# Self-attention scores as two 64-row tiles in two PSUM banks, with one bank for the output tiles

## The reference

```python
q = (x @ wq).reshape(b, s, 32, 16)      # 32 query heads of width 16
k = (x @ wk).reshape(b, s, 8, 16)       # 8 key groups
v = (x @ wv).reshape(b, s, 8, 16)
k = repeat(k, 4); v = repeat(v, 4)
scores = einsum('bihd,bjhd->bhij', q, k) * 16 ** -0.5
scores = where(causal, scores, min)
out = einsum('bhij,bjhd->bihd', softmax(scores), v).reshape(b, s, 512)
x = x + out @ wo
```

## Time and profile before

| | us |
|---|---|
| median of three runs | 1805.7 (1804.93 to 1806.73) |
| the profiled execution | 1809.07 |
| its span in the profile | 1807.3 |

### The profile page before, as it was taken

How to read it: one execution, slowest core, us unless ns; L and a number is a source line. 1 busy time by engine, 2 the same in 40 slices (tenths; PEclk the granted TensorE clock), 3 DMA queues, 4 the chain that set the end, 5 groups by cost and what they waited for, 6 DMA issues and landing times.

```text
span 1807.3 us, 29658 instructions
## 1 busy us (share of the span) xinstructions
PE 1719.4 (95%) x11352; PEld 1386.4 (77%) x11352; DVE 944.6 (52%) x1657; ACT 749.7 (41%) x1332; POOL 656.1 (36%) x511
## 2 busy tenths in 40 slices
PE   6899899999999999989988998999999999999998
PEld 5556688888888888778974567888888888887797
DVE  4388354544444545574544873544545444446643
ACT  2485344343444444431225753443443434444221
POOL 3396223233242332460115942233232332425500
PEclk9899899999999999999998998999999999999999
DMA  4110011010110101120111100110101201101000
GB/s 164 53 36 7 18 42 29 29 58 17 41 41 17 58 17 46 37 81 31 52 59 47 42 1 18 42 47 29 41 27 31 58 17 41 41 24 58 31 19 24
DMA packets 25871, 70.92 MB, mean 39 GB/s; under 512 B 3152, under 2 KB 3152, under 8 KB 25808
## 3 DMA queue, kind: packets, MB, share of 16 engines
q1 hardware_dynamic: 25808, 70.05, 12.5%
HBM read 65.85 MB, written 4.19 MB: 39 GB/s over the span
## 4 chain that ended last, share of the span: by engine, by line
PE 82%; DVE 7%; ACT 5%; POOL 4%; issue 2%; DMA 0%; POOLq 0%; SPq 0%; DVEq 0%; ACTq 0%
PE acc L391 15%; PE acc L393 13%; PE acc L392 13%; PE y L391 8%; PE y L393 8%; PE y L392 8%; PE sc L642 4%; PE ot L656 4%; PE acc L409 3%; PE pt L432 2%; ACT kt L990 2%; PE acc L625 1%; POOL prob L1576 1%; POOL prob L1582 1%; PE sc L568 1%
## 5 line engine op out<-in xcount | busy, mean ns | idle before, releaser
L1563 POOL TENSOR_TENSOR w_lo<-stage,w_hi 128x1024 fp32r<-128x1024 f32 (+1 forms) x88 | 171.6, 1961 | 281.7 <-ACT w_hi L810 281.7
L1576 POOL TENSOR_TENSOR prob<-prob,pmax 128x512 f32<-128x512 f32 x128 | 133.5, 1043 | 353.4 <-DVE pmax L1182 353.4
L391 PE MATMUL acc<-w_hi,xn_hi 128*128 128x512 f32 (+1 forms) x576 | 227.8, 396 | 11.2 <-DVE xn_lo L1140 11.2
L391 PE MATMUL y<-w_hi 128*128 128x512 f32 x576 | 237.0, 411 | 0.9 <-issue 0.9
L393 PE MATMUL y<-w_hi,w_lo 128*128 128x512 f32 x576 | 225.9, 392 | 0.0
L392 PE MATMUL y<-w_lo,w_hi 128*128 128x512 f32 x576 | 224.9, 390 | 0.0
L393 PE MATMUL acc<-w_hi,xn_lo 128*128 128x512 f32 (+1 forms) x576 | 220.4, 383 | 0.0
L392 PE MATMUL acc<-w_lo,xn_hi 128*128 128x512 f32 (+1 forms) x576 | 220.1, 382 | 0.0
L1140 DVE TENSOR_TENSOR w_lo<-ot,w_hi 128x1024 fp32r<-128x1024 f32 (+1 forms) x80 | 89.3, 1117 | 208.1 <-ACT w_hi L1001 207.8
L1567 POOL TENSOR_TENSOR qkrs<-qkve,mhalf 128x10 f32<-128x10 f32 x64 | 125.0, 1953 | 152.5 <-DVE qkve L1271 152.5
L1582 POOL TENSOR_TENSOR prob<-prob,prec 128x512 f32<-128x512 f32 x128 | 147.6, 1153 | 89.7 <-DVE prec L1190 89.4
(11 more groups left out here) (129 smaller groups left out, 3666.7 us busy)
## 6 DMA issues: line engine op xcount, KB each, us to landing
stage<-in_w_cross SPq DMA_DIRECT2D x64, 512.0 KB, 3.6
stage<-in_w_cross SPq DMA_DIRECT2D x32, 256.0 KB, 2.7
stage<-in_w_ffn SPq DMA_DIRECT2D x16, 512.0 KB, 3.5
x<-in_x SPq DMA_DIRECT2D x8, 512.0 KB, 3.7
stage<-in_w_self SPq DMA_DIRECT2D x8, 512.0 KB, 4.5
kt<-in_ctx SPq DMA_DIRECT2D x16, 256.0 KB, 2.6
out_x<-x SPq DMA_DIRECT2D x16, 256.0 KB, 2.0
stage<-in_w_self SPq DMA_DIRECT2D x4, 256.0 KB, 3.2
```

Of the source, the lines that this page charges most:

```text
L391: nc.tensor.matmul(target, l_hi, r_hi, start=first, stop=False)
L1563: nc.gpsimd.tensor_tensor(low, stage[:, place.slot(n), 0:width], high.bitcast(F32), ALU.subtract).then_inc(w_lo_done, 1)
L1576: nc.gpsimd.tensor_tensor(pr, pr, spread(pmax[:, buffer, :], 8, SEQ), ALU.subtract).then_inc(s_sub.sem, 1)
```

## The change

`sc` and the old bank `y1` become one pair `sy`. In a self-attention unit bank 0 takes key groups 0 to 3 (contraction rows 0 to 63) and bank 1 groups 4 to 7 (rows 64 to 127), 256 columns each. The keys are spread over four groups only: the selector's two halves are added, so that `kbd[:, 0:4]` holds groups 0 to 3 in the upper 64 rows and 4 to 7 in the lower. Since bank 1 is taken by scores, tiles 0 to 6 are all projected into `y0`, two heads in each second iteration (from u = 9 on), and tile 7 alone into bank 1 after the loop. The first head of a tile now waits for the update of the tile just before it. On DVE the update moves to the front of its turn, and that of tile 5 into turn 34.

```diff
-        sc = bank("sc")
+        sy = stack.enter_context(nc.psum_tensor("sy", [P, 2, COLS], F32))
+        sc = sy[:, 0, :]
+        y0 = bank("y0")
+        y = [y0[:], sy[:, 1, :]]
...
-            def project_part(at, i, made, h):
+            def project_part(at, i, made, h, bank_no, freed):
...
-                    pe.wait_ge(y_free.sem, at(y_free, i - 1))
+                    pe.wait_ge(y_free.sem, at(y_free, freed))
...
-                    nc.tensor.matmul(sc[:], ident_r[:], causal_r[:].rearrange("p g k -> p (g k)"),
-                                     start=True, stop=False)
-                    nc.tensor.matmul(sc[:], q1t[:, b, 2 * rp:2 * rp + 2, :].rearrange("p r q -> p (r q)"),
-                                     kbd[:, b % 2].rearrange("p g k -> p (g k)"), start=False, stop=True
-                                     ).then_inc(sc_rdy.sem, 1)
+                    if u == 0:
+                        pe.wait_ge(y_free.sem, at(y_free, 0))
+                    for part in range(2):
+                        nc.tensor.matmul(sy[:, part, 0:256], ident_r[:], causal_r[:, 0:4].rearrange("p g k -> p (g k)"),
+                                         start=True, stop=False)
+                    for part in range(2):
+                        half_rows = slice(part * SEQ, (part + 1) * SEQ)
+                        ins = nc.tensor.matmul(sy[:, part, 0:256],
+                                               q1t[half_rows, b, 2 * rp:2 * rp + 2, :].rearrange("p r q -> p (r q)"),
+                                               kbd[half_rows, b % 2, 0:4].rearrange("p g k -> p (g k)"),
+                                               start=False, stop=True)
+                    ins.then_inc(sc_rdy.sem, 1)
...
-                    if u >= 8:
-                        project_part(at, (u - 8) // 4, (u - 8) // 4 + 1, u % 4)
+                    if u >= 8 and u % 2:
+                        i = (u - 8) // 4
+                        for h in (u % 4 - 1, u % 4):
+                            project_part(at, i, i + 1, h, 0, i)
...
-                for h in range(1, REP):
-                    project_part(at, 6, 7, h)
+                for h in range(REP):
+                    project_part(at, 6, 7, h, 0, 6)
...
-                    nc.scalar.copy(prob[:, u % PRING, :], sc[:]).then_inc(s_add.sem, 1)
+                    nc.scalar.copy(prob[:, u % PRING, :].rearrange("p (b c) -> p b c", b=2), sy[:, :, 0:256]
+                                   ).then_inc(s_add.sem, 1)
...
-                    nc.vector.tensor_tensor(kbd[:, b % 2], kt[:, b * SEQ:(b + 1) * SEQ].unsqueeze(1).to_broadcast(
-                        [P, NG, SEQ]), spread(gsel[:], NG, SEQ), ALU.mult).then_inc(kbd_done.sem, 1)
+                    nc.vector.tensor_tensor(kbd[:, b % 2, 0:4], kt[:, b * SEQ:(b + 1) * SEQ].unsqueeze(1).to_broadcast(
+                        [P, 4, SEQ]), spread(gsel[:, 0:4], 4, SEQ), ALU.mult).then_inc(kbd_done.sem, 1)
...
                 for w in range(UNITS1 + 4):
+                    if w >= 16 and w % 4 == 0:
+                        updated((w - 16) // 4)
...
-                    if w >= 16 and w % 4 == 0:
-                        updated((w - 16) // 4)
+                    if w == UNITS1 + 2:
+                        updated(5)
...
-                updated(5)
...
+                nc.gpsimd.tensor_tensor(gsel[:, 0:4], gsel[:, 0:4], gsel[:, 4:8], ALU.add).then_inc(const_made.sem, 1)
```

36 lines of the change are left out of this document (18 added, 18 removed).

## The result

The changed kernel takes 1814.45 us (median of five runs, 1812.21 to 1815.83) against 1806.73 for the kernel before, run beside it: a ratio of 1.0044, 95% interval 1.0029 to 1.0059. It is **slower by 7.7 us**, where 3.8 us faster was forecast. Lines of kernel.py have moved by 3 to 17: the scores are L573 and L578, the head matmuls L394 to L396, the transposes of xn L412, the spread of the keys L1309, the update of x L1215, GpSimd's piece of w_lo L1580.

The account below looks back on a forecast made before the run. TensorE ends most waits, with GpSimd and VectorE close behind. Per half -1.8 (cold start) -2.2 (middle) +2.1 (end of pass) = -1.9, -3.8 for both, from 1805.7 to 1801.9 us; range 1797 to 1808.

Parts of the forecast that it names:

- Part 1: Self-attention score matmul as two 64-row tiles: 0.78 us with turns instead of 0.86, a gain of 0.08 per unit.
- The cross-attention block: Existing 64-row tiles of the same type and 256 columns, two pairs in 1.07 us; used to price the score pair.
- The first rival: Score tiles at full speed: turns vanish, TensorE leaves the path; -5.7 us per half, 1794.3; chance 0.10.
- Part 2: Two output-projection heads in each second unit: gain 0.11 us, loss 0.12 in two units, net 0.
- Part 3: Keys spread over four groups: VectorE's multiply 0.92 to about 0.46 us; per four units DVE -0.9, POOL -0.45.
- part 4: One output bank: a tile's first head waits for VectorE's update; 0.7 us of cover, cost 0 to 0.2 a tile.
- The last rival: Single output bank is waited for: 0.9 us at ten tile handovers, 9 us, giving 1810.9; chance 0.13.
- Part 5: End of pass: tile 6's heads stand behind the xn transpose, TensorE idles 2.0 us; +2.1 per half.
- The third rival: Clock falls in the new idle at the end of the pass: 1.65 us lost per half, 1805.2; chance 0.13.
- The cold start: First units of a pass at 1.2 GHz: three intervals gain 0.5 us each, -1.8 per half (bounds 1.2 and 2.9).
- The clock also rises sooner: Start of a pass: the condition given for the larger bound, a gain of 2.9 us per half.
- the 0.2 of GpSimd's collisions: Stretch before 96.36: 0.2 us gained from GpSimd's collisions, within the middle's sum of 2.2 per half.

Follow-up runs that it names:

- onebank_warm: Kernel before with one output bank and heads paired, plus added TensorE matmuls in the cold-start waits: 1809.02 us.
- after: The changed kernel itself, all parts of the change against the kernel before: 1814.45 us, ratio 1.0044.
- keys_first: Changed kernel with the spread of the keys ahead of the update of x in turns 16, 20, 24, 28: 1809.66 us.
- full_height: Changed kernel with both score matmuls of a unit on all 128 rows instead of 64 each: 1815.62 us.
- one_bank: Changed kernel with scores in one bank, 512 columns over 128 rows, and keys spread over all 512 columns: 1820.25 us.
- after_warm: Changed kernel, both new VectorE orders kept, plus added TensorE matmuls in the cold-start waits: 1809.11 us.
- before_warm: Kernel before plus added TensorE matmuls in the waits of its cold start: 1804.58 us.
- both_orders: Changed kernel with old VectorE orders: key spread before the update of x, tile 4's normalization before tile 5's update: 1805.84 us.

## Why the prediction was wrong, step by step

- **Part 1, the tile pair: right.** Forecast were 0.64 for the pair, 0.09 ahead of it and a gain of 0.08 a unit. Measured were 0.64, 0.09 to 0.12 ahead, 0.06 behind in the transposes (0.05 forecast), and a gain of 0.105. PE's demand for two units is 5.39 and 5.40 were forecast. The cross-attention block was the right row. The first rival (tiles at full speed) is refuted: of the 2x that the Trainium skill allows (TensorEngine Tiling (Array Packing), Theoretical Speedup) the scores kept 0.86 to 0.64, and the causal pair gave some of it back.
- **Part 2, the pairing, net 0: too low.** With the single bank it costs 4.4 us in all. In onebank_warm the four units of a half with a handover take 4.08 to 4.46 where their like take 3.56, 2.4 us of waits for DVE's update in a half, and a pair of units at the full clock is 5.59 against 5.54.
- **Part 3, the spread: right in the main.** Its median went from 0.97 to 0.65, a gain of 0.3 where 0.46 was forecast. The 0.92 that I halved was the time of a spread that met a GpSimd operation; with none running it is 0.69 in the kernel before and 0.41 to 0.43 after. GpSimd's operation beside it takes 1.23 instead of 1.49. The step as a whole (two banks, half the columns) is worth 5.8 us.
- **The first failed step: part 4 moves the update to the front of its turn and puts no price on it.** It pushes the spread 1.7 us later on DVE, and I never asked what of GpSimd stands there; part 3 had priced only the spread's meeting with GpSimd's short operation ("I take 0.22 of that 0.44 back"). It was an operation of 2.39 us, and the spread took all of it. Units 16 to 24 were to gain 0.9 and lost 1.4.
- **Part 4, the wait for the single bank: right for the kernel as changed.** No first head in the loop waits there. The danger was real: without the unit that pairing frees, and with DVE's old order, the wait is 2.56 and the kernel takes 1839.0. The last rival had the mechanism, but it acts in another kernel.
- **Part 5, the end of the pass: right.** Forecast +2.1 per half and 2.0 of idle, measured 2.13 and 2.04. The third rival (the clock falls in the idle) came true in one half of the profile, at 1.6 where it gave 1.65. Its chance of 0.13 was too low: of the ten such idles in the profiles of after, keys_first, full_height, one_bank and after_warm, six were followed by a fall, one in each of the first four programs and both in the last.
- **The cold start, -1.8 per half: the second failed step.** The interval at half clock fell from 3.24 to 2.70, as said (0.5 each), and in the second half the eight units gained 1.06. In the first half they lost 2.81. "The clock also rises sooner" was the only way in which I let the clock move, and how the bounds 1.2 and 2.9 came about is not worked out there. That a start at half clock can last longer was in no bound. It lasted 23.89 us in the first half, against 13.65 before and 10.24 in the second half of both kernels; why is not known.
- **The sum.** Forecast and result are 11.5 us apart (-3.8 and +7.7), in the profiled spans 10.1 (1807.3 and 1813.6). In the profiles 5.7 us of it are the two starts (-2.0 each with the 0.2 of GpSimd's collisions, against +2.81 and -1.06). 2.4 are the rest of the passes up to the last score (-2.0 each, against -1.26 and -0.33). 1.7 are the end of the second pass, where the clock fell. 1.8 lie ahead of the first pass (its first score is at 76.15, not 74.38), where one more stretch at half clock stands around 38 us. The profile of before_warm, which has nothing of the change, has that stretch too, so it need not come from the change. These make 11.6; the other 1.5 has the opposite sign and lies behind the two passes. By the medians with the added matmuls the weights are others: the starts of the passes are 2.3 and the two orders 10.6. What was left out were the neighbours of a moved operation and the clock on its bad side.

## What to carry to other kernels

When an operation moves in its engine's queue, lay the other engines' timelines beside the new place, not the old one: a 0.65 us operation of VectorE lasted until the GpSimd operation of 2.39 us that it ran into was over. A buffer given up has to be paid for with a gap in which its reader can finish, so price the gap together with the buffer. And where a pass starts at half clock with TensorE waiting, price both ways in which the clock may go, or fill the waits: that alone was worth 3 us to the kernel before and 7.4 to both_orders.

## What the runs showed of the hardware

- A VectorE multiply of two tensors in SBUF, the spread over 256 columns, took 0.37 to 0.43 us when no GpSimd operation was running as it began. Begun beside one of 1.04 it took 0.59 to 0.75 in the changed kernel, and 2.31, 2.32 and 1.88 beside one of 2.39. In each of these collisions it ended 0.28 us after the GpSimd operation, however early it had begun; the spread over 512 columns in the kernel before mostly ended 0.55 after it. The xn of one tensor ended 0.28 after it too: 0.55 alone, 1.26 beside an operation of 1.04.
- Reductions of one tensor kept their 0.67 to 0.69 beside GpSimd operations, and the update of x, with one operand in PSUM, its 0.64 to 0.69.
- At the low clock, PE busy 12.00 of 12.00 us was not answered by a rise in one pass (88 to 100), while in another pass of nearly the same program the clock was back by 88. No experiment here says what decides it.
- At the full clock, two fp32 matmuls of 64 rows and 256 columns side by side cost 0.64, and two of 128 rows and 256 columns 0.86, as much as one of 512. The causal matmuls ahead of the 64-row pair cost 0.09 to 0.12 more than ahead of the full-height one, and the transposes behind it 0.06 more.
